# Causal attention: the maxima of the diagonal blocks masked on VectorE instead of by band matmuls on TensorE

## The chip, the core and the metric

The program runs on one core of one Trainium2 chip. The metric is the time of one execution in microseconds of device time, the median of several runs; each comparison is made on one chip. The engines are TensorE (PE in the profile, its weight loads PEld), VectorE (DVE), ScalarE (ACT), GpSimd (POOL) and SyncE (SP), which here only issues DMAs. Each has its own queue, and they wait for one another by semaphores.

## What is computed

Two transformer layers of model width 256 on 4096 tokens: causal attention with 16 heads of 16 dimensions over a 64-wide latent, an MLP with fp4 rounding, full attention, and a coupling network, with a layer norm behind each. The change is in the first attention. Cut to what matters:

```python
def _L0_attn_ref(x, W_q, W_dkv, W_uk, W_uv, W_o, ln_gamma, ln_beta):
    ...                                   # q, k, v: (1, 16, 4096, 16), q and k rotated
    scores = jnp.einsum('bhqd,bhkd->bhqk', q, k) / jnp.sqrt(jnp.float32(HEAD_DIM))
    causal = jnp.tril(jnp.ones((t, t), dtype=bool))
    scores = jnp.where(causal[None, None], scores, -jnp.inf)
    attn = jax.nn.softmax(scores, axis=-1)
    out = jnp.einsum('bhqk,bhkd->bhqd', attn, v)
```

All is float32. The softmax needs each query's maximum over the keys up to its own.

## The kernel before

The function `attention` (L1042) makes both attention layers; `causal` is true for the first. Four heads form a group, 512 queries a block; a **unit** is one block of one group, 32 in the causal layer. The first group takes its blocks from the shortest (512 keys) to the longest (4096), the other three from the longest to the shortest.

For each unit the scores are computed twice. First for the maxima: queries on the partitions, keys along the columns. A **set** is one tile of 128 queries, one pair of heads and 512 keys (`take_max`, L1345): two matmuls (L1353), one for each head of the pair, into two banks of `ps`. VectorE takes the maximum along the columns of both banks in one operation (`reduce_max`, L1503, the reduce at L1506). There are two pairs of banks, used in turn: TensorE waits on `max_taken` until the set two before has been reduced, VectorE on `max_scored`. When all sets of a unit are done, the **gather** (L1510) takes the maximum over the chunks of 512 keys, negates it and splits it in two parts; TensorE turns it (L1363), ScalarE copies it out, and SyncE writes it into extra rows of the queries, so that the second score matmul subtracts it.

Second for the values: keys on the partitions (L1407), `exp` on ScalarE (L1483), and the values matmuls (L1447). A **half-step** is one tile of 128 keys and two of the four heads: two score matmuls, the values matmuls of an earlier tile, and whatever sets of maxima of a coming unit the plan has put between them. The plan (`order`, L1149) is a list that all engines follow; a table of costs (`half_cost`, `max_cost`) spreads the sets over the half-steps so that each unit's maxima are ready some time before the unit begins.

A set is **diagonal** when its keys are those of the unit's own block. Its width is then (qt + 1) x 128 columns for query tile qt, 128 to 512, and in the last 128 columns keys later than the query must not count. Each unit has eight such sets (four tiles, two pairs), and they come last, in a row, ahead of the gather: a **burst**. The band does the masking: after the two score matmuls four more with bfloat16 operands (`add_band`, L1341, the matmul at L1343) add a matrix with -1e30 above the diagonal to those 128 columns, in two halves of 64 rows for each of the two banks:

```python
if diagonal:
    for m in range(2):
        for b in range(2):
            mm = add_band(bank(b)[:, qt * P:wide], b, m)
```

`pick` and `band` are made by GpSimd at the start of the layer (L1277 to L1287), and TensorE waits for them there (`ones_set`, L1367). The probabilities on the diagonal are masked separately, after the exp, by GpSimd (L1293).

Of the kernel before, what the change touches and what calls it, by code (L numbers as in the profile page):

```python
# [1041 lines left out]
def attention(nc, core, ps, ident, layer, causal, q_parts, k_parts, v_dram, K, o_all):  # L1042
# [147 lines left out]
    def par_of(u):  # L1190
        return group_of(u) % 2
# [29 lines left out]
    with ExitStack() as ctx:  # L1221
# [11 lines left out]
        if causal:  # L1233
            pick = sb("pick", [P, 2, P], BF16)
            band = sb("band", [P, 2, P], BF16)

# [36 lines left out]
        with nc.Block() as block:  # L1273
            if causal:
                @block.gpsimd
                def _(pool):
                    pool.memset(band[:], 0.0).then_inc(ones_set, 1)  # L1277
                    pool.memset(pick[:], 0.0).then_inc(ones_set, 1)
                    pool.wait_ge(ones_set, 2)
                    for b in range(2):  # L1280
                        rows = slice(b * HALF, (b + 1) * HALF)
                        for m in range(2):

                            pool.affine_select(out=pick[rows, m], in_=pick[rows, m], compare_op=ALU.not_equal, fill=1.0,
                                               base=m * HALF, pattern=[[-1, P]], channel_multiplier=1).then_inc(ones_set, 1)
                            pool.affine_select(out=band[rows, m], in_=band[rows, m], compare_op=ALU.is_ge, fill=MASKED,
                                               base=m * HALF, pattern=[[-1, P]], channel_multiplier=1).then_inc(ones_set, 1)  # L1287
                    pool.wait_ge(ones_set, 10)
                    for u in range(UNITS):
                        for kt in range(keys(u) - QT, keys(u)):  # L1290
                            pool.wait_ge(emptied, last_score(u, kt) + 4)
                            square = probs[:, (n_key[u] + kt) % PBUFS, :, width(u, kt):width(u, kt) + P]
                            pool.affine_select(out=square, in_=square, compare_op=ALU.is_ge, fill=0.0, base=0,  # L1293
                                               pattern=[[0, GH], [1, P]], channel_multiplier=-1).then_inc(masked, 1)
# [45 lines left out]
            def _(pe):  # L1340
                def add_band(dst, b, m):  # L1341
                    rows = slice(b * HALF, (b + 1) * HALF)
                    return pe.matmul(dst, pick[rows, m], band[rows, m], start=False, stop=(m == 1))  # L1343

                def take_max(i, u, at, pair):  # L1345
# [5 lines left out]
                    for b in range(2):  # L1351
                        rows = slice(b * HALF, b * HALF + SROWS)
                        mm = pe.matmul(bank(b)[:, 0:wide], Q[rows, slot_of(u), j, qt * P:(qt + 1) * P],  # L1353
                                       K[rows, par_of(u), j, c * QB:c * QB + wide], start=True, stop=not diagonal)
                    if diagonal:
                        for m in range(2):
                            for b in range(2):
                                mm = add_band(bank(b)[:, qt * P:wide], b, m)
                    mm.then_inc(max_scored, 1)
# [5 lines left out]
                pe.sem_inc(values_done, PBUFS)  # L1365
                if causal:
                    pe.wait_ge(ones_set, 10)  # L1367
                pe.wait_ge(q_got[slot_of(0)], 96)
# [133 lines left out]
            def _(dve):  # L1502
                def reduce_max(i, u, at, pair):  # L1503
                    j, qt, c = maxima(u)[i]
                    dve.wait_ge(max_scored, at + 1)
                    dve.tensor_reduce(mx[:, u % 2, :, j, qt, c],  # L1506
                                      ps[:, 2 + 2 * pair:4 + 2 * pair, 0:max_width(u, i) // 2], AX.X,
# [771 lines left out]
```

## Time and profile before

| | |
|---|---|
| time, median of 3 runs | 5093.4 us (5091.18 to 5099.55) |
| the profiled execution | 5093.37 us, its span 5091.6 us |
| TensorE busy | 4866.5 us, 96% of the span |
| VectorE busy | 4444.5 us, 87% |
| ScalarE busy | 3780.7 us, 74% |
| GpSimd busy | 376.3 us |
| causal layer | about 160 to 1670 us |
| reduces of the maxima, both layers | 3200, 3729.7 us of VectorE |
| band matmuls | 1024, 80.6 us of TensorE |

The time of an execution is the span, from the first to the last instruction, and a little around it. Busy time of TensorE says less than it seems: its matmuls overlap and their ends are modelled, so the time that a group adds to the program is read from the distance of the steps in the timeline. The same holds on a smaller scale for VectorE, where an operation may start while the one before is still ending: the distance of two starts is the price, the duration is what a waiting engine sees. "Idle before" is the time an engine stood still ahead of an instruction, and behind the arrow stands who ended it.

### The profile page before, as it was taken

The page shows a single profiled execution, that of the slowest core. Times are in us where ns is not written, and L with a number is a line of the kernel's source. Part 1 is how long each engine was busy: PE and PEld are TensorE (multiplying, and loading weights), DVE is VectorE, ACT ScalarE, POOL GpSimd, SP SyncE. Part 2 cuts the span into 40 slices and gives each one's busy share as a digit, 9 for nine tenths or more (in the row PEclk, how much of TensorE's full clock was granted, in tenths as well). Part 3 has the DMA queues.
Part 4 walks back from the last instruction along what each step waited for, and adds up shares of the span by engine and source line. Part 5 has one row for each costly group of instructions (what it writes and reads, how often), then busy time and mean ns, then how long its engine had stood idle before and what let it go on. Part 6 is the DMA issues. An engine that isn't in the chain of part 4 may idle for free. (4 is left out here: it accounts for less than half of the span.)

```text
span 5091.6 us, 102136 instructions
## 1 busy us (share of the span) xinstructions
PE 4866.5 (96%) x42155; PEld 1991.5 (39%) x42155; DVE 4444.5 (87%) x5051; ACT 3780.7 (74%) x7192; POOL 376.3 (7%) x546
## 2 busy tenths in 40 slices
PE   8799999999999899869999999999999999999998
PEld 5333333333334465523333333333333333333443
DVE  7799988988876599489999999999999999998346
ACT  3377888887878433318888888888888888888853
POOL 4100000000000233300000000000000000000120
PEclk9699999999999899959999999999999999999999
DMA  6301010010000000531000010000100000000000
GB/s 192 93 11 38 8 41 8 14 42 11 11 8 2 16 14 8 182 72 37 9 7 5 8 37 9 8 5 8 38 8 8 5 8 5 8 5 2 9 1 33
DMA packets 138405, 131.34 MB, mean 26 GB/s; under 512 B 61748, under 2 KB 96852, under 8 KB 137940
## 3 DMA queue, kind: packets, MB, share of 16 engines
q1 hardware_dynamic: 128964, 118.95, 7.9%
q10 hardware_dynamic: 8976, 5.86, 0.8%
q8 instruction: 332, 5.44, 0.4%
q14 instruction: 133, 1.09, 0.1%
HBM read 76.75 MB, written 46.66 MB: 24 GB/s over the span
## 5 line engine op out<-in xcount | busy, mean ns | idle before, releaser
L1506 DVE TENSOR_REDUCE att_mx<-ps 128x2 f32<-128x1024 f32 (+2 forms) x3200 | 3729.7, 1192 | 252.8 <-PE ps L1353 159.4
L1483 ACT ACTIVATE att_probs<-ps 128x512 f32<-128x512 f32 (+3 forms) x6400 | 3379.8, 583 | 576.0 <-PE ps L1407 262.4
L1447 PE MATMUL ps<-att_probs,att_V 128*17 128x256 f32 (+1 forms) x24576 | 1913.8, 386 | 0.4 <-ACT att_outT L1499 0.2
L1407 PE MATMUL ps<-att_Q,K 50*128 50x512 f32 (+3 forms) x6272 | 1618.1, 490 | 24.1 <-ACT att_probs L1483 23.1
L1353 PE MATMUL ps<-K,att_Q 48*128 48x512 f32 (+3 forms) x6400 | 1364.6, 409 | 83.9 <-DVE att_mx L1506 50.9
L1407 PEld LDWEIGHTS ps<-att_Q,K 50*128 50x128 f32 x6272 | 628.4, 184 | 1320.6 <-ACT att_probs L1483 1227.9
L1447 PEld LDWEIGHTS ps<-att_probs,att_V 128*17 128x17 f32 x24576 | 415.6, 95 | 1025.1 <-issue 564.7
L1353 PEld LDWEIGHTS ps<-K,att_Q 48*128 48x128 f32 x6400 | 645.1, 191 | 166.4 <-DVE att_mx L1506 120.1
L1842 POOL MEMSET mix_power<- 128x1 f32 x1 | 0.1, 99 | 2643.0 <-POOLq L132 2643.0
L1293 POOL TENSOR_SCALAR_AFFINE_SELECT att_probs<-att_probs 128x512 f32<-128x512 f32 x128 | 81.6, 638 | 1454.1 <-ACT att_probs L1483 1454.1
L1634 PE MATMUL ps<-wguT,mlp_xqT 128*128 128x512 f32 (+1 forms) x384 | 159.7, 566 | 0.0
L1673 ACT ACTIVATE mlp_gate<-ps 128x704 f32<-128x704 f32 x32 | 24.2, 757 | 138.8 <-PE ps L1634 138.8
L1462 ACT ACTIVATE att_negT<-ps 32x128 fp32r<-32x128 f32 x65 | 17.2, 265 | 128.4 <-PE ps L1363 123.7
L1541 DVE RECIPROCAL att_rden<-att_out 128x16 f32<-128x16 f32 (+1 forms) x65 | 16.4, 252 | 104.5 <-ACT att_out L1492 104.4
L1634 PEld LDWEIGHTS ps<-wguT,mlp_xqT 128*128 128x128 f32 x384 | 71.8, 194 | 71.8 <-issue 63.3
L1652 PE MATMUL ps<-wdT,mlp_hqT 128*128 128x256 f32 (+1 forms) x384 | 95.6, 391 | 0.6 <-DVE mlp_y L1731 0.6
L2081 PE MATMUL ps<-xT_all,net_w 128*128 128x512 f32 x192 | 95.6, 621 | 0.0
L2029 DVE TENSOR_SCALAR cn_cf<-cn_th,cn_ab 128x512 f32<-128x512 f32 x24 | 13.1, 546 | 83.5 <-ACT cn_th L2163 83.0
L1652 PEld LDWEIGHTS ps<-wdT,mlp_hqT 128*128 128x128 f32 (+1 forms) x384 | 71.0, 192 | 26.3 <-issue 11.6
L1343 PE MATMUL ps<-att_band,att_pick 64*128 64x128 bf16 x1024 | 80.6, 234 | 0.0
L2145 ACT ACTIVATE cn_h<-ps,net_b 128x512 f32<-128x512 f32 x48 | 33.0, 687 | 57.8 <-PE ps L2081 57.8
L591 DVE TENSOR_TENSOR proj_qprod<-ps,proj_tabT 128x1024 f32<-128x1024 f32 x16 | 18.8, 1220 | 50.6 <-PE ps L437 50.6
(213 smaller groups left out, 2463.2 us busy)
## 6 DMA issues: line engine op xcount, KB each, us to landing
att_Q<-qhi_scratch SPq DMA_DIRECT2D x252, 64.0 KB, 2.3
K<-khi_scratch SPq DMA_DIRECT2D x212, 64.0 KB, 2.3
v_scratch<-proj_vpad SPq DMA_DIRECT2D x16, 544.0 KB, 4.4
att_Q<-qlo_scratch SPq DMA_DIRECT2D x126, 64.0 KB, 2.3
att_V<-v_scratch SPq DMA_DIRECT2D x53, 136.0 KB, 2.4
K<-klo_scratch SPq DMA_DIRECT2D x106, 64.0 KB, 2.3
att_Q<-att_negT SPq DMA_DIRECT2D x260, 4.0 KB
proj_x<-in_L_attn_x SPq DMA_DIRECT2D x8, 512.0 KB, 6.2
```

Of the source, the lines that this page charges most:

```text
L1293: pool.affine_select(out=square, in_=square, compare_op=ALU.is_ge, fill=0.0, base=0, pattern=[[0, GH], [1, P]], channel_multiplier=-1).the ...
L1343: return pe.matmul(dst, pick[rows, m], band[rows, m], start=False, stop=(m == 1))
L1353: mm = pe.matmul(bank(b)[:, 0:wide], Q[rows, slot_of(u), j, qt * P:(qt + 1) * P], K[rows, par_of(u), j, c * QB:c * QB + wide], start=True, ...
L1407: mm = pe.matmul(ring(at)[:, lo:QB], K[rows, par_of(u), j, kt * P:(kt + 1) * P], Q[rows, slot_of(u), j, lo:QB], start=True, stop=True)
L1447: mm = pe.matmul(ps[VW * h:VW * h + HV, 6, lo:(part + 1) * (QB // 2)], V[:, par_of(v), kt, HV * h:HV * (h + 1)], probs[:, (n_key[v] + kt) ...
L1483: act.activation(probs[:, (n_key[u] + kt) % PBUFS, h if half_wide(u) else column(h), lo:QB], ring(at)[:, lo:QB], ACT.Exp, scale=SCALE).the ...
L1506: dve.tensor_reduce(mx[:, u % 2, :, j, qt, c], ps[:, 2 + 2 * pair:4 + 2 * pair, 0:max_width(u, i) // 2], AX.X, ALU.max).then_inc(max_taken, 1)
L1634: mm = pe.matmul(gu_ps[:, b:to], xqT[:, par, c, :], wguT[:, c, b:to], start=(c == 0), stop=(c == DC - 1))
L1652: mm = pe.matmul(down, hqT[0:kw, par, k, :], wdT[0:kw, k, :], start=(k == 0), stop=(k == NK - 1))
L1673: act.activation(gate[:], gate_ps, ACT.Silu).then_inc(s["gate_kept"], 1)
L2081: mm = pe.matmul(bank1(k, m), nets.w1[:, c, m * P:(m + 1) * P], xT_all[:, c, cols_of(k)], start=(c == 0), stop=(c == DC - 1))
L2145: act.activation(h1[:, k % 2, m], bank1(k, m), ACT.Gelu, bias=nets.b1[:, m:m + 1]).then_inc(s["hid1"], 1)
```

## The change

The band matmuls and the matrices `pick` and `band` are gone. Instead GpSimd makes one row mask `future` (128 x 512, bfloat16): zero in its first 384 columns and -1e30 above the diagonal of its last 128. For a diagonal set VectorE now runs one `tensor_tensor_reduce` for each of the two banks: it adds the last `wide` columns of `future` to the bank, writes the sum back into the bank and takes its maximum. TensorE signals the set after its two score matmuls. The wait for GpSimd's mask moves from TensorE to VectorE. The other sets, the plan and its costs are as before.

```diff
--- before.py
+++ after.py
@@ -1231,8 +1231,7 @@
         negT = sb("negT", [PARTS * NEG, 2, P], F32R)
         rden = sb("rden", [P, QT, GH])
         if causal:
-            pick = sb("pick", [P, 2, P], BF16)
-            band = sb("band", [P, 2, P], BF16)
+            future = sb("future", [P, QB], BF16)
 
         ones_set = core.sem(pre + "ones_set")
         k_first = [core.sem(f"{pre}k_first_{i}") for i in range(NQB)]
@@ -1274,18 +1273,11 @@
             if causal:
                 @block.gpsimd
                 def _(pool):
-                    pool.memset(band[:], 0.0).then_inc(ones_set, 1)
-                    pool.memset(pick[:], 0.0).then_inc(ones_set, 1)
-                    pool.wait_ge(ones_set, 2)
-                    for b in range(2):
-                        rows = slice(b * HALF, (b + 1) * HALF)
-                        for m in range(2):
-
-                            pool.affine_select(out=pick[rows, m], in_=pick[rows, m], compare_op=ALU.not_equal, fill=1.0,
-                                               base=m * HALF, pattern=[[-1, P]], channel_multiplier=1).then_inc(ones_set, 1)
-                            pool.affine_select(out=band[rows, m], in_=band[rows, m], compare_op=ALU.is_ge, fill=MASKED,
-                                               base=m * HALF, pattern=[[-1, P]], channel_multiplier=1).then_inc(ones_set, 1)
-                    pool.wait_ge(ones_set, 10)
+                    pool.memset(future[:], 0.0).then_inc(ones_set, 1)
+                    pool.wait_ge(ones_set, 1)
+
+                    pool.affine_select(out=future[:, QB - P:QB], in_=future[:, QB - P:QB], compare_op=ALU.is_ge, fill=MASKED,
+                                       base=0, pattern=[[-1, P]], channel_multiplier=1).then_inc(ones_set, 1)
                     for u in range(UNITS):
                         for kt in range(keys(u) - QT, keys(u)):
                             pool.wait_ge(emptied, last_score(u, kt) + 4)
@@ -1338,10 +1330,6 @@
 
             @block.tensor
             def _(pe):
-                def add_band(dst, b, m):
-                    rows = slice(b * HALF, (b + 1) * HALF)
-                    return pe.matmul(dst, pick[rows, m], band[rows, m], start=False, stop=(m == 1))
-
                 def take_max(i, u, at, pair):
                     j, qt, c = maxima(u)[i]
                     pe.wait_ge(max_taken, at + 1)
@@ -1351,11 +1339,7 @@
                     for b in range(2):
                         rows = slice(b * HALF, b * HALF + SROWS)
                         mm = pe.matmul(bank(b)[:, 0:wide], Q[rows, slot_of(u), j, qt * P:(qt + 1) * P],
-                                       K[rows, par_of(u), j, c * QB:c * QB + wide], start=True, stop=not diagonal)
-                    if diagonal:
-                        for m in range(2):
-                            for b in range(2):
-                                mm = add_band(bank(b)[:, qt * P:wide], b, m)
+                                       K[rows, par_of(u), j, c * QB:c * QB + wide], start=True, stop=True)
                     mm.then_inc(max_scored, 1)
 
                 def turn_max(count, at):
@@ -1363,8 +1347,6 @@
                     pe.transpose(ring(at)[:, 0:P], negp[:], ident[:]).then_inc(scored, 1)
 
                 pe.sem_inc(values_done, PBUFS)
-                if causal:
-                    pe.wait_ge(ones_set, 10)
                 pe.wait_ge(q_got[slot_of(0)], 96)
                 keys_here, values_here = set(), set()
 
@@ -1503,6 +1485,16 @@
                 def reduce_max(i, u, at, pair):
                     j, qt, c = maxima(u)[i]
                     dve.wait_ge(max_scored, at + 1)
+                    if on_diagonal(u, c):
+                        if u == 0:
+                            dve.wait_ge(ones_set, 2)
+                        wide = (qt + 1) * P
+                        for b in range(2):
+                            ins = dve.tensor_tensor_reduce(ps[:, 2 + 2 * pair + b, 0:wide], ps[:, 2 + 2 * pair + b, 0:wide],
+                                                           future[:, QB - wide:QB], 1.0, MASKED, ALU.add, ALU.max,
+                                                           mx[:, u % 2, b, j, qt, c:c + 1])
+                        ins.then_inc(max_taken, 1)
+                        return
                     dve.tensor_reduce(mx[:, u % 2, :, j, qt, c],
                                       ps[:, 2 + 2 * pair:4 + 2 * pair, 0:max_width(u, i) // 2], AX.X,
                                       ALU.max).then_inc(max_taken, 1)
```

On VectorE, the first unit's eight diagonal sets at the start of the layer, before (`att_mx` holds the maxima, `att_neg` and `att_negp` the gather's results):

```order
L1506 TENSOR_REDUCE att_mx<-ps 128x2 x8
L1513 TENSOR_REDUCE att_neg<-att_mx 128x16
L1517 CAST att_negp<-att_neg 128x16
L1518 TENSOR_TENSOR att_negp<-att_neg,att_negp 128x16
L1506 TENSOR_REDUCE att_mx<-ps 128x2 x16
```

and now, the last of the eight sets and the gather behind it:

```order
L1493 ISA ps,att_mx<-ps,att_future 128x512
L1493 ISA att_mx 128x1
L1493 ISA ps,att_mx<-ps,att_future 128x512
L1493 ISA att_mx 128x1
L1505 TENSOR_REDUCE att_neg<-att_mx 128x16
L1509 CAST att_negp<-att_neg 128x16
L1510 TENSOR_TENSOR att_negp<-att_neg,att_negp 128x16
L1498 TENSOR_REDUCE att_mx<-ps 128x2 x16
```

The one operation in the code is two instructions in the program, one that reads and writes the bank and one that writes a single column, the maximum: a diagonal set is four instructions where it was one reduce.

On TensorE, in the fifth unit's burst, a half-step with a full set and the two narrowest diagonal sets, before (`K` and `att_Q` are keys and queries, `att_probs` the exponentials):

```order
L1407 MATMUL ps<-att_Q,K 128x512 x2
L1353 MATMUL ps<-K,att_Q 128x512 x2
L1353 MATMUL ps<-K,att_Q 128x128 x2
L1343 MATMUL ps<-att_band,att_pick 128x128 x4
L1353 MATMUL ps<-K,att_Q 128x128 x2
L1343 MATMUL ps<-att_band,att_pick 128x128 x4
L1447 MATMUL ps<-att_probs,att_V 17x256 x4
```

and now:

```order
L1389 MATMUL ps<-att_Q,K 128x512 x2
L1341 MATMUL ps<-K,att_Q 128x512 x2
L1341 MATMUL ps<-K,att_Q 128x128 x4
L1429 MATMUL ps<-att_probs,att_V 17x256 x4
L1389 MATMUL ps<-att_Q,K 128x512 x2
```

Nothing else has moved: the sets stand in the same half-steps, and only the groups of four band matmuls are missing between them.

## Rows read from the trace of the kernel before

**Rows 1.** The page: span; busy us (share of span) xinstructions of each engine
```profile
span 5091.6 us, 102136 instructions
...
PE 4866.5 (96%) x42155; PEld 1991.5 (39%) x42155; DVE 4444.5 (87%) x5051; ACT 3780.7 (74%) x7192; POOL 376.3 (7%) x546
```

**Rows 2.** Busy us by stretches of the causal layer, then granted clock, DMA
```profile
160.00:480.00 320.00, 298.39 (x2654) 122.47 (x2653) 295.51 (x302) 207.47 (x418) 15.30 (x24) 0.89 0.16 39
480.00:1320.00 840.00, 820.77 (x8283) 325.06 (x8283) 751.56 (x747) 682.73 (x1362) 42.76 (x67) 0.99 0.07 19
1320.00:1670.00 350.00, 343.28 (x3375) 137.92 (x3373) 256.66 (x258) 287.78 (x581) 18.48 (x29) 0.98 0.02 6
```

**Rows 3.** Groups by shape, 160 to 1670 us: busy, mean ns | idle before
```profile
L1506 DVE TENSOR_REDUCE att_mx<-ps 128x2 f32<-128x1024 f32 x960 | 1140.5, 1223 | 122.6 <-PE ps L1353 100.2 <-PE ps L1343 18.6
...
L1343 PE MATMUL ps<-att_band,att_pick 64*128 64x128 bf16 x1021 | 80.4, 234 | 0.0
...
L1506 DVE TENSOR_REDUCE att_mx<-ps 128x2 f32<-128x768 f32 x64 | 60.3, 957 | 24.2 <-PE ps L1343 23.8
...
L1506 DVE TENSOR_REDUCE att_mx<-ps 128x2 f32<-128x256 f32 x64 | 26.9, 423 | 15.2 <-PE ps L1343 15.0
```

**Rows 4.** Waits, 160 to 1670 us: who for whom, total us, times, longest
```profile
DVE att_mx L1506 <- PE ps L1343: 87.2, 137, 8.5
...
PE ps L1353 <- DVE att_mx L1506: 26.6, 55, 1.1
```

**Rows 5.** Timeline, TensorE, unit 8's burst: start, us, instructions [idle before]
```profile
574.94 0.33 PE L1353 MATMUL ps<-K,att_Q 48*128 48x128 f32 x2 [0.76 <-DVE att_mx L1506]
...
580.01 0.51 PE L1407 MATMUL ps<-att_Q,K 50*128 50x512 f32 x2
...
581.37 0.50 PE L1407 MATMUL ps<-att_Q,K 50*128 50x512 f32 x2
...
582.73 0.50 PE L1407 MATMUL ps<-att_Q,K 50*128 50x512 f32 x2
...
583.95 0.50 PE L1407 MATMUL ps<-att_Q,K 50*128 50x512 f32 x2
...
585.56 0.49 PE L1353 MATMUL ps<-K,att_Q 48*128 48x512 f32 x2
```

**Rows 6.** Timeline of VectorE, the same burst and behind its gather
```profile
568.76 6.46 DVE L1506 TENSOR_REDUCE att_mx<-ps 128x2 f32<-128x1024 f32 x6 [1.17 <-PE ps L1353]
...
580.92 2.58 DVE L1506 TENSOR_REDUCE att_mx<-ps 128x2 f32<-128x1024 f32 x2 [0.40 <-PE ps L1343]
...
584.28 5.75 DVE L1506 TENSOR_REDUCE att_mx<-ps 128x2 f32<-128x1024 f32 x5
```

**Rows 7.** Timeline of VectorE, unit 7's burst
```profile
485.51 8.56 DVE L1506 TENSOR_REDUCE att_mx<-ps 128x2 f32<-128x1024 f32 x8
...
497.22 4.29 DVE L1506 TENSOR_REDUCE att_mx<-ps 128x2 f32<-128x768 f32 x4 [0.61 <-PE ps L1343]
```

**Rows 8.** Timeline of TensorE, behind unit 7's gather
```profile
503.57 0.49 PE L1353 MATMUL ps<-K,att_Q 48*128 48x512 f32 x2
```

**Rows 9.** Timeline of VectorE, short operations of the MLP
```profile
1901.69 0.43 DVE L1731 TENSOR_TENSOR mlp_y<-ps,a_all 128x256 f32<-128x256 f32 x1 [0.42 <-PE ps L1652]
1902.03 0.41 DVE L1731 TENSOR_TENSOR mlp_y<-ps,mlp_x 128x256 f32<-128x256 f32 x1
...
1903.24 0.27 DVE L1741 TENSOR_SCALAR mlp_var<-mlp_mv 128x1 f32<-128x1 f32 x2
1903.44 0.89 DVE L174 TENSOR_REDUCE mlp_qh_amax<-mlp_h 128x44 f32<-128x704 f32 x1
```

**Rows 10.** Timeline of all engines, the start of the causal layer
```profile
151.10 0.48 DVE L1522 MEMSET ps<- 128x512 f32 x1
...
153.29 0.30 POOL L1286 TENSOR_SCALAR_AFFINE_SELECT att_band<-att_band 64x128 bf16<-64x128 bf16 x1
...
159.31 0.47 PE L1353 MATMUL ps<-K,att_Q 48*128 48x128 f32 x2 [11.03 <-DMA K<-khi_scratch]
```

## Prediction

> **What bounds the kernel now.** I read the page first [rows 1]: TensorE is busy 96% of the span, VectorE 87%, ScalarE 74%. That is an average over stages, so next came the busy time by stretches [rows 2]. The change touches only the causal layer, which runs from 160 to about 1670 us. In its first 320 us VectorE is busy 296 of 320 us and TensorE 298; from 480 to 1320 TensorE has 821 of 840 and VectorE 752; in the last 350 us VectorE has 257 and TensorE 343. So TensorE sets the pace, and VectorE is close behind it until 1320. The granted clock is 0.89, 0.99 and 0.98 there; I assume that it stays so.
>
> Then the groups of the layer by shape [rows 3]: 960 full reduces of 1223 ns, and 64 each for three, two and one quarter of the width, 957 to 423 ns. The 256 diagonal sets are those 192 and 64 of the full ones. The band's 1021 recorded matmuls are 80.4 us busy, but busy is not cost here, since matmuls overlap. The waits [rows 4] show both sides: VectorE waited 87.2 us for the band's line (137 times, 8.5 us of it once, at the start), TensorE 26.6 us for VectorE's reduces. Diagonal sets come eight in a row, one burst in each of 32 units, and what the change does is decided inside the bursts and just behind them.
>
> **What the band costs TensorE.** In the timeline of unit 8's burst [rows 5] a half-step (two score matmuls, one set of maxima, eight values matmuls) with a full-width diagonal set runs from 580.01 to 581.37 and from 581.37 to 582.73: 1.36 us. The next one, without a band, 582.73 to 583.95, takes 1.22. So a band of four matmuls costs 0.14 us of TensorE's pace, a sixth of what 4 x 234 ns suggests; 256 sets give 36 us. That is the most that the change can take off.
>
> **What VectorE gets.** One reduce over two banks becomes, by the built order, four instructions: per bank an add-and-maximum and a one-column write of its result. No row of before shows either, so both are bounded by neighbours, in start-to-start time, since that is what a queue of them costs. The reduces: five full ones in a row take 5.75 us [rows 6], so they start (5.75 - 1.22)/4 = 1.13 apart although each lasts 1.22; a quarter more, 2 x 128 columns, costs 0.267 (1223 - 957) [rows 3]. So the old sets cost 0.33, 0.60, 0.87 and 1.13, and a burst 5.86. Nearest to the new main instruction is the tensor-tensor that reads a bank: 256 columns, 0.43 long, the next starts 0.34 later (1901.69, 1902.03) [rows 9]; with the same slope that is 0.21, 0.34, 0.47 and 0.61 for 128 to 512 columns. Nearest to the one-column write are the one-column tensor-scalars: two of them, and the next row starts 0.20 later (1903.24, 1903.44), 0.10 each [rows 9]. Bounds: from below 0.06, if a write without an input is cheaper than these; from above each instruction at its full length, no overlap, 0.16 fixed for a main one (0.43 - 0.267) and 0.15 for a write (0.27 for two that overlap). I take 0.34 and 0.10, the rows nearest in shape. A set then costs 2 x (bank + 0.10) = 0.61, 0.88, 1.15, 1.41, a burst of eight 8.10: **2.24 us more per unit**, 72 us over the stage. VectorE's waits in the bursts, 87.2 - 8.5 = 79 us, are of that size: it can be carried, if it falls in the right places.
>
> The Trainium skill ("VectorE: DVE Perf Modes", Rules for kernel authors) asks to keep the number of VectorE operations low and speaks against turning one into four. Its page on this has no price for the second instruction; nothing below needs it.
>
> **Two bursts worked through.** Rules, from the rows: TensorE writes a set 0.05 after the reduce two sets earlier has ended (two pairs of banks); VectorE may start 0.04 after the last matmul; a reduce's end is seen 0.08 after the next may start.
> Unit 8 [rows 5, 6]: the first diagonal reduce starts at 574.80, inside the row of six. With the new costs the eight start at 574.80, 575.41, 576.34 (waits for its matmuls), 577.22, 578.10, 579.25, 580.40, 581.81 and the last ends at 583.30, against 583.50. TensorE, without bands, starts the half-step behind the burst at 581.78 instead of 582.73: it is 0.95 ahead. But the gather (0.77 from the last reduce to the first full one) now starts with VectorE a set behind, the first full reduce ends at 585.28, and TensorE's third set behind the burst, which needs its banks, goes at 585.33 instead of 585.56. Of 1.1 us saved 0.23 is left: **-0.23**.
> Unit 7 [rows 7, 8] is denser: the planner, whose costs are unchanged, puts three small sets in one half-step and the last four reduces run without a gap. The same working gives 493.66, 494.27, 494.88, 495.83, 496.98, 498.13, 499.28, 500.69, an end at 502.18 (before about 501.51), a first full reduce until 504.16, and TensorE's write at 504.21 instead of 503.57: **+0.64**.
>
> **The sum.** Counting the 32 bursts of the timeline by VectorE's idle time in them: 11 are like unit 8 (1.9 to 2.7 us idle), 8 like unit 7 (1.4 to 1.5), 2 (the first units of the last two head groups) have 0.9 and lose about 1.1 each. The first four units run at a lower clock, where the band is dearer and VectorE waits 1.2 to 3.2 us; I put them at 0, give or take 2. In the last seven VectorE has room (257 of 350 us, [rows 2]) and most of 8 x 0.14 stays, 0.9 each. 11 x -0.23 + 8 x 0.64 + 2 x 1.1 + 0 - 7 x 0.9 = -2.5 + 5.1 + 2.2 - 6.3 = **-1.5 us**.
> Edits at nothing: the mask's preparation on GpSimd shrinks from ten operations to two, but it was done by 153.6 and the first maxima matmul at 159.31 waited for a key load [rows 10]; without that load it would save about 2 us. The wait for it moves to VectorE, which has nothing to do then. The second layer, projections and MLP are unchanged.
> The profiled execution took 5093.37 us with a span of 5091.6, the median is 5093.4: so 5093.4 - 1.5 = **5092 us**.
> Sensitivity: some 25 bursts have 16 pairs each, so 0.01 us more per pair costs up to 4 us. With 0.08 for the write it is 5084, with 0.12 5100.
>
> **Rivals.**
> 1. *Not slower, but faster: VectorE's room suffices.* If the one-column write is nearly free (0.06 and less, as a write without input), a unit-8 burst leaves TensorE 0.9 us ahead and a unit-7 burst is even. 16 us and more off; at the limit all 36: 5058 to 5082, say 5074. The point from which it decides is about 0.08 per write. For it: the 79 us of waits. Against: the one-column rows that there are take 0.10.
> 2. *Slower: the four instructions don't overlap.* A write of the accumulated maximum may hold the next until the main one has drained. Then each pair costs 0.08 + 0.05 more, 25 x 16 x 0.13 = 52 us, less what bursts with room absorb: **5144**; half of it (only the write waits) 5115. For it: the write depends on the instruction ahead of it, which no pair in [rows 9] does. Against: every row of VectorE shown overlaps its successor by about 0.08. The Trainium skill says two things here ("VectorE: DVE Perf Modes"): under The DRAIN you can't avoid, that the next operation waits until the pipe is empty, which would be this rival; under Two Vector instructions with no wait between them, that one which isn't held starts earlier, which is my forecast. The five reduces 1.13 apart side with the second, for reduces.
> 3. *Reading and writing the same bank halves the rate.* Nothing in before does both. A unit's eight sets hold 2560 columns in two banks each, 2560 x 1.04 ns x 2 = 5.3 us more: some 28 bursts, 150 us, 5240. Against: the one VectorE write into a bank takes 0.48 us for 512 columns [rows 10], no slower than a read.
>
> **How the numbers follow.** About 0.2% (10 us) is what a measurement of this kernel can tell from no change. Forecast (within 0.2%, 5083 to 5104): 0.40. Rival 1: 0.26. Rival 2 from its half on, with prices between: 0.29. Rival 3: 0.05. The range runs from 5070 to 5148: it leaves out rival 3, the deep end of rival 1 and a tail of rival 2, some 0.18. So faster 0.26, same 0.40, slower 0.34.
>
> **What would show it.** Two new groups on VectorE, 512 each: a main one of about 0.29 to 0.69 us and a one-column one whose successor starts 0.10 later (right), 0.06 or less (rival 1), 0.15 and more or with gaps (rival 2); a main one of 512 columns over 1.1 us is rival 3. VectorE's busy time in the layer should rise by 70 to 100 us. TensorE's half-steps with a full diagonal set should be 1.22 where VectorE keeps up; its waits for VectorE's line, 26.6 us, should grow to some 40 to 60, right behind the gathers. If they stay at 27, the write is cheap; if they pass 90, rival 2 or 3 holds. The prediction is wrong altogether if the last 350 us of the layer don't get shorter, since there TensorE alone should decide.

## The result: 0.2 to 0.4% slower, because TensorE's granted clock fell

The changed kernel takes 5125.2 us in the median of 5 runs (5113.4 to 5130.1) against 5093.4 of 5 runs before: ratio 1.0043, 95% interval 1.0022 to 1.0064. Ten more runs of it, beside 22 of before, gave 5115.2 us and 1.0021 (1.0007 to 1.0034). The forecast was 5092, within 0.2%. Four runs of the experiments, far above the others of their kernel (5166 us in e1, 8147 in e10, 10099 in e3, 12741 in e13), are left out of every figure below. The profiled execution took 5113.4 us. Its page (span; then busy us, share, instructions) answers to [rows 1]:

```profile
span 5111.7 us, 100847 instructions
...
PE 4872.8 (95%) x41131; PEld 1972.0 (39%) x41131; DVE 4483.7 (88%) x5819; ACT 3781.4 (74%) x7192; POOL 373.5 (7%) x538
```

The 1024 band matmuls are gone, VectorE has 39 us more, TensorE 6 us more busy time although it does less. The stretches of the layer, as in [rows 2], the granted clock third from the end:

```profile
160.00:480.00 320.00, 292.70 (x2346) 114.53 (x2345) 295.40 (x462) 199.78 (x404) 15.23 (x24) 0.85 0.17 39
480.00:1320.00 840.00, 815.61 (x7573) 310.77 (x7571) 760.26 (x1139) 673.32 (x1334) 38.72 (x61) 0.96 0.07 19
1320.00:1670.00 350.00, 341.90 (x3180) 133.57 (x3176) 275.26 (x429) 287.76 (x584) 19.67 (x31) 0.97 0.03 7
```

0.89, 0.99 and 0.98 have become 0.85, 0.96 and 0.97. The records of the granted clock know two levels only, 2.4 and 1.2 GHz: stretches at the lower one that begin between 160 and 1690 us add up to 58 us before and 154 us after. The second layer and the MLP are as they were.

**What VectorE does now** (groups by shape, 160 to 1691 us: busy, mean ns of one | idle before), for [rows 3]:

```profile
L1498 DVE TENSOR_REDUCE att_mx<-ps 128x2 f32<-128x1024 f32 x896 | 1062.9, 1222 | 114.2 <-PE ps L1341 112.7
L1493 DVE CUSTOM_DVE_ANT_0 ps<-ps,att_future 128x512 f32<-128x512 f32 x128 | 85.4, 724 | 11.8 <-PE ps L1341 10.8
L1493 DVE DVE_READ_ACCUMULATOR2_ANT att_mx<- 128x1 f32 x512 | 72.4, 141 | 0.0
...
L1493 DVE CUSTOM_DVE_ANT_0 ps<-ps,att_future 128x128 f32<-128x128 f32 x128 | 33.8, 314 | 8.6 <-PE ps L1341 8.3
```

What counts in a queue is the distance of the starts. In unit 8's burst (timeline, VectorE: start, us):

```profile
583.29 0.29 DVE L1493 CUSTOM_DVE_ANT_0 ps<-ps,att_future 128x128 f32<-128x128 f32 x1
...
588.71 0.70 DVE L1493 CUSTOM_DVE_ANT_0 ps<-ps,att_future 128x512 f32<-128x512 f32 x1
589.33 0.14 DVE L1493 DVE_READ_ACCUMULATOR2_ANT att_mx<- 128x1 f32 x1
589.33 0.73 DVE L1493 CUSTOM_DVE_ANT_0 ps<-ps,att_future 128x512 f32<-128x512 f32 x1
589.98 0.14 DVE L1493 DVE_READ_ACCUMULATOR2_ANT att_mx<- 128x1 f32 x1
589.98 0.73 DVE L1493 CUSTOM_DVE_ANT_0 ps<-ps,att_future 128x512 f32<-128x512 f32 x1
```

The one-column read starts together with the next main instruction. From main to main it is 0.65 us at 512 columns, and over all pairs 0.25, 0.38, 0.52 and 0.65 us for 128 to 512. The trace does not divide a pair between its two instructions; it is 0.04 us over the price that the prediction gave the main instruction alone, so with that price the read costs 0.04, not 0.10. A burst is 7.2 us, not 8.1.

**And TensorE in that burst** (timeline):

```profile
589.16 0.50 PE L1389 MATMUL ps<-att_Q,K 50*128 50x512 f32 x2
...
590.37 0.50 PE L1389 MATMUL ps<-att_Q,K 50*128 50x512 f32 x2
...
591.59 0.50 PE L1389 MATMUL ps<-att_Q,K 50*128 50x512 f32 x2
...
593.47 0.50 PE L1341 MATMUL ps<-K,att_Q 48*128 48x512 f32 x2 [0.16 <-DVE att_mx L1498]
```

Half-steps with a full diagonal set take 1.21 and 1.22 us, as forecast. From the first diagonal instruction on VectorE (583.29) to TensorE's third set behind the burst it is 10.18 us, against 10.76 in [rows 5, 6] (574.80, inside the row of six, to 585.56): 0.58 us gained. Here the clock is at its full level throughout (columns as in [rows 2]):

```profile
580.00:597.00 17.00, 15.85 (x155) 6.04 (x151) 16.28 (x43) 13.33 (x27) 0.59 (x1) 1.00 0.01 1
```

So in this burst the work itself got cheaper, and the time went elsewhere.

**Where it went.** Gathers mark the units. The gathers of units 23 and 24 before (timeline, VectorE):

```profile
1233.59 0.18 DVE L1513 TENSOR_REDUCE att_neg<-att_mx 128x16 f32<-128x16 f32 x1
...
1318.59 0.29 DVE L1513 TENSOR_REDUCE att_neg<-att_mx 128x16 f32<-128x128 f32 x1
```

and after:

```profile
1249.83 0.18 DVE L1505 TENSOR_REDUCE att_neg<-att_mx 128x16 f32<-128x16 f32 x1
...
1342.49 0.29 DVE L1505 TENSOR_REDUCE att_neg<-att_mx 128x16 f32<-128x128 f32 x1
```

The distance grew from 85.0 to 92.7 us. In this run the 7.7 us fall together with one long stretch at the lower clock, shown here with a shorter one ahead of it (busy time by stretches of after; columns as in [rows 2]):

```profile
1228.00:1231.40 3.40, 2.40 (x24) 1.00 (x26) 2.90 (x11) 1.48 (x4) 0.00 (x0) 1.00 0.00 0
1231.40:1238.20 6.80, 6.80 (x46) 2.29 (x38) 4.43 (x17) 4.08 (x8) 0.00 (x0) 0.50 0.01 2
...
1248.40:1251.80 3.40, 2.83 (x28) 1.16 (x20) 3.26 (x11) 2.94 (x6) 0.00 (x0) 1.00 0.45 113
1251.80:1275.70 23.90, 23.90 (x133) 7.93 (x133) 13.36 (x13) 12.82 (x25) 0.00 (x0) 0.50 0.01 3
```

At both falls TensorE had just paused: 2.40 of 3.40 us busy, then 2.83 of 3.40. At half clock it is busy without a gap, and the others wait for it (VectorE is busy 13.4 of 23.9 us). The Trainium skill ("TensorE: Matmul & The Clock Gate", What's actually happening) says that the gate between the two levels follows how busy the array has been; these rows agree as far as the falls stand behind pauses; that the clock stayed low through 23.9 us without a gap does not fit it, and here the measurement decides. Pauses alone are not enough, either. At the same places of the program, ahead of the gather of unit 22 and behind that of unit 23 (1240.5 and 1249.8 us in after, 1224.6 and 1233.6 in before), the kernel before pauses nearly as much and keeps its clock:

```profile
1214.00:1217.40 3.40, 2.53 (x32) 1.29 (x28) 2.80 (x4) 1.52 (x3) 0.00 (x0) 1.00 0.00 0
...
1234.40:1237.80 3.40, 2.93 (x23) 1.14 (x21) 3.31 (x3) 3.28 (x8) 0.00 (x0) 1.00 0.09 29
```

**Time against clock.** Each run has its mean granted clock beside its time, and the runs of one kernel differ in both. The 135 runs of before that went with the experiments reach from 5083.9 us at 0.968 to 5130.2 us at 0.958. One straight line with a common slope and a level for each of the 19 kernels fits 301 runs to 3.2 us (the spread around it): **3.9 us for 0.001 of clock**. That splits each difference into what the work costs at an equal clock (0.962, by the line) and what the clock adds. Times and clocks below are medians; each ratio is to the runs of before on the same chip. "Two-byte" counts the matmuls in the band's form and type. The experiments ran at six times on five chips, each time beside before, whose mean clock came out at 0.964 or 0.965 and whose level by the line at 5112 to 5118 us; so differences of level below some 6 us between kernels of different times say little.

| kernel | two-byte matmuls | plan | us | ratio (95%) | clock | us at 0.962 |
|---|---|---|---|---|---|---|
| before | 1024 | old | 5103.0 | 1 | 0.965 | 5114 |
| after (15 runs) | 0 | old | 5117.7 | 1.0043, 1.0021 | 0.958 | 5103 |
| e1 no band, old reduces | 0 | old | 5094.3 | 0.9989 (0.9970 to 1.0008) | 0.960 | 5087 |
| e2 band and new reduces | 1024 | old | 5117.4 | 1.0030 (1.0012 to 1.0047) | 0.963 | 5122 |
| e3 after, planned | 0 | new | 5089.8 | 0.9977 (0.9963 to 0.9991) | 0.961 | 5086 |
| e4 before, half band | 512 | old | 5110.7 | 1.0013 (0.9990 to 1.0037) | 0.960 | 5104 |
| e5 as e1, half reduces | 0 | old | 5078.5 | 0.9954 (0.9930 to 0.9978) | 0.962 | 5080 |
| e6 e3 + 2 score-like on diagonal | 0 | new | 5114.7 | 1.0027 (1.0006 to 1.0049) | 0.960 | 5108 |
| e7 e3 + 2 score-like elsewhere | 0 | new | 5109.1 | 1.0009 (0.9982 to 1.0035) | 0.961 | 5105 |
| e8 after + band in ten units | 320 | old | 5129.2 | 1.0035 (1.0014 to 1.0057) | 0.958 | 5113 |
| e9 e3 + band in ten units | 320 | new | 5093.1 | 0.9979 (0.9964 to 0.9993) | 0.964 | 5101 |
| e10 after + 4 score-like (3 runs) | 0 | old | 5219.4 | 1.0238 (1.0175 to 1.0301) | 0.943 | 5148 |
| e11 e3 + 4 zeros on diagonal | 1024 | new | 5094.3 | 0.9991 (0.9976 to 1.0007) | 0.966 | 5110 |
| e12 e3 + 4 zeros elsewhere | 896 | new | 5091.6 | 0.9985 (0.9968 to 1.0001) | 0.9665 | 5110 |
| e13 after, planned wider | 0 | wider | 5088.7 | 0.9971 (0.9953 to 0.9990) | 0.963 | 5092 |
| e14 e3 + 2 zeros elsewhere | 448 | new | 5096.1 | 0.9976 (0.9958 to 0.9994) | 0.963 | 5101 |
| e15 e3 + 4 short zeros elsewhere | 896 | new | 5091.0 | 0.9971 (0.9949 to 0.9992) | 0.964 | 5099 |
| e16 e3 + 4 four-byte zeros elsewhere | 0 | new | 5130.2 | 1.0043 (1.0021 to 1.0066) | 0.9595 | 5120 |
| e17 after + 4 zeros elsewhere | 896 | old | 5142.9 | 1.0062 (1.0044 to 1.0079) | 0.958 | 5126 |

At an equal clock the change gains 5114 - 5103 = 11 us (13 in the ten runs of e0 against the runs of before beside them). Its clock is 0.0066 lower in the mean (0.9580 of 15 runs, 0.9646 of 135), which costs 26 us.

### The profile page after: what moved, and what is told of

Its sections match the earlier page's. It is cut to its first block and busy times, and to the rows that moved or that the text cites. A ratio compares the mean times of both kernels' runs of the same rounds, so it can differ in the third digit from the quotient of the medians.

```text
span 5111.7 us, 100847 instructions
## 1 busy us (share of the span) xinstructions
PE 4872.8 (95%) x41131; PEld 1972.0 (39%) x41131; DVE 4483.7 (88%) x5819; ACT 3781.4 (74%) x7192; POOL 373.5 (7%) x538
## 5 line engine op out<-in xcount | busy, mean ns | idle before, releaser
L1498 DVE TENSOR_REDUCE att_mx<-ps 128x2 f32<-128x1024 f32 x2944 | 3525.8, 1224 | 175.1 <-PE ps L1341 172.0
L1429 PE MATMUL ps<-att_probs,att_V 128*17 128x256 f32 (+1 forms) x24576 | 1933.4, 389 | 0.2
L1493 DVE CUSTOM_DVE_ANT_0 ps<-ps,att_future 128x384 f32<-128x384 f32 (+3 forms) x512 | 237.2, 520 | 57.4 <-PE ps L1341 55.4
L1493 DVE DVE_READ_ACCUMULATOR2_ANT att_mx<- 128x1 f32 x512 | 72.4, 141 | 0.0
```

The source lines that it names most:

```text
L1429: mm = pe.matmul(ps[VW * h:VW * h + HV, 6, lo:(part + 1) * (QB // 2)], V[:, par_of(v), kt, HV * h:HV * (h + 1)], probs[:, (n_key[v] + kt) ...
L1493: ins = dve.tensor_tensor_reduce(ps[:, 2 + 2 * pair + b, 0:wide], ps[:, 2 + 2 * pair + b, 0:wide], future[:, QB - wide:QB], 1.0, MASKED, A ...
L1498: dve.tensor_reduce(mx[:, u % 2, :, j, qt, c], ps[:, 2 + 2 * pair:4 + 2 * pair, 0:max_width(u, i) // 2], AX.X, ALU.max).then_inc(max_taken, 1)
```

## Experiments: which part of the change moves the clock

**e0**, the changed kernel again.

> The changed kernel itself, for the spread of its granted clock over more runs. If its slowness is the clock: single runs spread over 30 us or more and each lies on one line of time against clock, 3.9 us for 0.001; the median clock is 0.954 to 0.959, that of before 0.965. If the first five runs were chance: a median clock of 0.962 or above and 5085 to 5105 us.

5105.3 to 5129.5 us, clock 0.955 to 0.962, median 0.9595: a spread of 24 us, not 30, and a median clock just above what was expected of the first theory, well below the 0.962 of the second. The slowness stands, and the runs lie on the common line of time against clock.

**e1 and e2** take the two halves of the change apart. e1 removes the band and leaves VectorE its old reduces; e2 keeps the band and has the new instructions.

```diff
 e1: after, and in reduce_max
-                    if on_diagonal(u, c):
...
-                        return
 e2: before, and in reduce_max
+                    if on_diagonal(u, c):
...
+                        return
```

> The band's matmuls are gone and VectorE keeps its old reduces; the diagonal sets' maxima are taken without the mask, which is left out. Before has a mean granted clock of 0.968, after 0.954 to 0.959. Theory P (pauses: the changed reduces hold TensorE up in the bursts, and its granted clock falls behind such pauses): nothing is added on VectorE, so the clock stays at 0.965 or above and 20 to 36 us come off, 5057 to 5073. Theory A (activity: the band's matmuls filled TensorE, and taking them away is what lowers the clock): the clock falls to 0.955 to 0.96 as in after, which takes 25 to 40 us back, 5075 to 5100. Theory V (VectorE's extra time alone costs the 20 to 30 us and the clock does not matter): 5057 to 5073, as P.

> The band's matmuls stay and VectorE takes the masked maxima in the new way as well (the mask is added twice, which leaves the probabilities as they are). Theory P: VectorE's longer bursts meet TensorE's longer ones, the pauses are like those of after or more, the clock falls to 0.96 or below, 5125 to 5160. Theory A: the band keeps the clock at 0.965 or above; the new reduces alone cost 0 to 0.6 us a unit, 5093 to 5112. Theory V: the clock stays at 0.965 or above and the time is 5130 to 5160, the extra of VectorE on top of the whole band.

e1: clock 0.960, 5094 us. Taking the band away lowers the clock with VectorE's work untouched: theory A, against P and V. At an equal clock the band is worth 5114 - 5087 = 27 us. e2: clock 0.963, between what A and P expected; the new instructions cost 5122 - 5114 = 8 us at an equal clock and some 0.001 of clock. TensorE's waits for VectorE do not separate the two (160 to 1690 us: us, times, longest). In e1:

```profile
PE ps L1341 <- DVE att_mx L1488: 30.0, 62, 1.3
```

and in e2:

```profile
PE ps L1358 <- DVE att_mx L1521: 25.7, 52, 1.1
...
PE ps L1358 <- DVE att_mx L1516: 4.6, 11, 0.6
```

30.0 and 30.3 us, and yet the profiled runs have 140 us at the lower clock in e1 and 48 in e2. Around the gather of unit 22 (1235.2 us in e2), where after fell first, e2 pauses about as much, twice, and holds (busy time by stretches):

```profile
1224.20:1227.60 3.40, 2.54 (x34) 1.13 (x28) 3.36 (x10) 1.75 (x4) 0.00 (x0) 1.00 0.00 0
...
1234.40:1237.80 3.40, 2.59 (x38) 1.29 (x38) 3.15 (x16) 1.53 (x4) 0.64 (x1) 1.00 0.03 7
```

**e3 and e13** tell the planner what a diagonal set costs now; e13 tells it more than that.

```diff
     def max_cost(u, i):
-        return 0.155 + max_width(u, i) / 960
+        return (0.31 if on_diagonal(u, maxima(u)[i][2]) else 0.155) + max_width(u, i) / 960
...
 e13: 0.6 in place of 0.31
```

> The changed kernel with one more fixed cost of 0.155 us for each diagonal set in the planner that spreads the sets over the half-steps (measured start distances of a pair, 0.249, 0.382, 0.515 and 0.649 us, make a set 0.50 to 1.30 us). A burst is then spread over more half-steps and VectorE is pressed less there. Theory P: fewer pauses, the clock goes back to 0.962 or above, 5065 to 5095. Theory A: as after, 0.954 to 0.959, 5113 to 5130. Theory V: TensorE waits less, 5080 to 5110 at an unchanged clock of 0.954 to 0.959.

> The changed kernel with a fixed cost of 0.6 us for each diagonal set in the planner in place of 0.31: the bursts are spread still wider, and VectorE has more room in them. Theory P (TensorE's pauses behind VectorE start the falls): fewer waits for VectorE, clock 0.962 or above, 5078 to 5090. Theory S: the clock stays at 0.961 and the time within 4 us of 5090, or above it, since the sets between the bursts are then closer together.

e3: 5089.8 us, faster than before by 0.23%. At an equal clock it is where e1 is (5086 and 5087, each to some 2 us): with bursts spread by their new price, the masked reduces cost no more than the old ones did in the old plan. (The old reduces were not run in the new plan.) The clock came half way, 0.961: spreading counts (P), but does not make up for the band. e13 has 0.963 and 5088.7, at an equal clock 6 us more than e3: it seems to gain clock and lose pace, but the two were run at different times, and the differences are at the edge of what can be told.

**e4 and e5.** Half of the band; and e1 with half of the columns reduced.

```diff
 e4: before, and in take_max
-                        for m in range(2):
+                        for m in range(1, 2):
 e5: e1, and in reduce_max
-                                      ps[:, 2 + 2 * pair:4 + 2 * pair, 0:max_width(u, i) // 2], AX.X,
+                                      ps[:, 2 + 2 * pair:4 + 2 * pair, 0:max_width(u, i) // (4 if on_diagonal(u, c) else 2)], AX.X,
```

> The kernel before with two of the four band matmuls of each diagonal set (the mask of the maxima reaches half of the query rows; the other half's maxima are taken unmasked). VectorE's work is as in before. Theory A (the band's matmuls keep TensorE's granted clock up; without them it fell to 0.960 in the median, with them 0.966): half of them hold it about half way, 0.962 to 0.964, and half of the 29 us that the band costs at an equal clock comes off: 5090 to 5102. Theory P (pauses behind VectorE lower the clock): as before, 0.966 and 5075 to 5087, since VectorE has no more to do. Theory N (the clock falls by chance, whatever the kernel): no order between the kernels' clocks.

> No band, and VectorE reduces only half of the columns of each diagonal set (the rest of these maxima is left out, and the mask): TensorE is not held up by VectorE inside a burst. Theory A: the clock stays low, 0.955 to 0.961, since TensorE has no more to do than without the band, 5075 to 5100. Theory P: the pauses are gone, the clock is 0.966 or above, 5050 to 5065.

e4 missed: its clock is not half way but at 0.960, though single runs reach 0.968. e5 has 0.962: relieving VectorE in the bursts gives back about 0.002, so pauses look like a smaller part, and without the band the clock does not return to 0.965.

**e6, e7, e10.** Is any matmul as good as the band's? Matmuls like those of the scores, on the set's own bank ahead of the real ones, overwritten by them; e6 and e10 on the diagonal, e7 off it.

```diff
+                    if diagonal:
+                        for b in range(2):
+                            rows = slice(b * HALF, b * HALF + SROWS)
+                            pe.matmul(bank(b)[:, 0:P], Q[rows, slot_of(u), j, qt * P:(qt + 1) * P],
+                                      K[rows, par_of(u), j, c * QB:c * QB + P], start=True, stop=True)
...
 e7: if causal and not diagonal and qt == 0; e10: the pair twice, old plan
```

> The changed kernel with the planner's new cost (median 5090 us at a clock of 0.9615), and in each diagonal set two more matmuls of 128 columns ahead of the real ones, whose results are overwritten (512 more matmuls, half as many as the band had). Theory A, any matmul counts: the clock comes back to 0.964 or above, which gives 10 to 15 us, and the matmuls cost about half of the band's 29 us: 5088 to 5096. Theory B (the band's own form counts): the clock stays at 0.961 and the matmuls' price is seen alone, 5100 to 5110.

> As the one before, but the two overwritten matmuls of 128 columns stand in the first quarter of the sets off the diagonal (224 sets, 448 matmuls), so away from the bursts where the band stood. Theory A, any place counts: the clock rises to 0.963 or above, 5085 to 5097. If only matmuls in the bursts count: the clock stays at 0.961 and the price is seen alone, 5098 to 5108.

> The changed kernel with four matmuls of 128 columns ahead of the real ones in every diagonal set, overwritten by these: as many as the band had, in its bursts, but in the form of the score matmuls. With the band itself in the same place the clock was 0.963 and the time 5117. Theory A1 (the number of matmuls in the bursts counts): clock 0.962 or above, 5117 to 5135. Theory A2 (the band's own form counts): clock 0.954 to 0.959, 5135 to 5165.

None brings the clock back: 0.960, 0.961, and 0.943 in the three runs of e10, below all others. Theory A in the form "any matmul counts" falls, and the times lie above the ranges given. Why e10 fell so far is open. In its profiled run the end of the causal layer, whose last gather is at 1752.5 us, ran almost wholly at the lower clock, 85 us in one stretch:

```profile
1690.00:1780.00 90.00, 88.35 (x588) 38.14 (x580) 24.80 (x80) 49.45 (x111) 8.88 (x14) 0.54 0.01 2
```

**e8 and e9.** The band beside VectorE's mask in ten units only.

```diff
+    def banded(u, c):
+        return on_diagonal(u, c) and (chunks(u) <= 2 or u <= 3)
...
-                    if diagonal:
+                    if banded(u, c):
```

> The changed kernel with the band's four matmuls kept besides (mask added twice) in the ten units that have at most two chunks of keys, or that are the third and fourth: 80 of 256 diagonal sets. Long stretches at the lower clock began at the ends of head groups, at 862 and 1234 us, where these units' bursts lie close together. Theory A (the band fills TensorE where it would pause, and the clock holds): the clock rises from 0.956 to 0.960 or above, and the band costs 8 us: 5108 to 5120. Theory B (the band has to stand everywhere): clock 0.954 to 0.959, 5120 to 5140.

> The same with the planner's new cost for diagonal sets (without the band: median 5090 us, clock 0.961). Theory A: clock 0.964 or above, 5078 to 5090, below every kernel so far. Theory B: clock 0.959 to 0.962, 5094 to 5102.

With the new plan the clock rises from 0.961 to 0.964, with the old one the median stays at 0.958 (the mean goes from 0.9580 to 0.9594). The time is no better, since the band costs what the clock gives.

**e11, e12, e16.** The band's matmuls without a mask: four that add zero, on the diagonal (e11) or in the first quarter of the sets off it (e12); in e16 as in e12, but with four-byte operands.

```diff
+                    if diagonal:
+                        for m in range(2):
+                            for b in range(2):
+                                rows = slice(b * HALF, (b + 1) * HALF)
+                                mm = pe.matmul(bank(b)[:, 0:P], future[rows, 0:P], future[rows, P:2 * P], start=False, stop=(m == 1))
...
 e12: if causal and not diagonal and qt == 0; e16: as e12, with a tile of four-byte zeros for future
```

> The changed kernel with the planner's new cost, and in each diagonal set four matmuls in the band's form (added to the set, 128 columns, two-byte operands) that add zero: the band's work without its mask. Without them: median 5090 us at 0.961. Theory F (matmuls in the band's form and place hold the clock): 0.964 or above; at an equal clock the band costs 26 us, so 5098 to 5108. Theory S (they do not; what holds the clock in the kernel before is that VectorE waits for the band, or chance): 0.959 to 0.962, 5110 to 5122.

> The same four matmuls that add zero, but in the first quarter of the sets off the diagonal (224 sets, 896 matmuls) and none on it. Theory F with the form alone: 0.964 or above, 5095 to 5105. Theory F with the place (only where bursts press VectorE): 0.959 to 0.962, 5108 to 5120. Two score-like matmuls in these places left the clock at 0.961.

> The four matmuls of zeros of 128 columns with operands in the type of the score matmuls (four bytes) in place of two bytes. If adding to a bank (not overwriting) or adding zeros is what holds the clock: 0.965 or above, 5090 to 5105. If the two-byte type is what holds it: 0.960 to 0.962, and the price of four-byte matmuls, 5110 to 5160.

The clearest answer of all: 0.966 and 0.9665, no run of either below 0.963, wherever the zeros stand; and 0.9595 for the same matmuls with the wider type. (Both zeros kernels are a little faster than theory F expected.) The groups of e12 and of e16 (busy us, mean ns) show that the wide ones keep TensorE busy no less:

```profile
L1347 PE MATMUL ps<-att_future 64*128 64x128 bf16 x896 | 71.0, 226 | 0.0
```

```profile
L1349 PE MATMUL ps<-att_nothing 64*128 64x128 f32 x896 | 85.2, 256 | 0.0
```

A part of the 256 ns is e16's lower clock itself. At an equal clock the wide zeros cost 34 us over e3, the two-byte ones 24.

**e14 and e15**: two zeros in place of four; four of 32 columns.

```diff
 e14: e12 with
-                        for m in range(2):
+                        for m in range(1):
 e15: e12 with
-                                mm = pe.matmul(bank(b)[:, 0:P], future[rows, 0:P], future[rows, P:2 * P], start=False, stop=(m == 1))
+                                mm = pe.matmul(bank(b)[:, 0:32], future[rows, 0:P], future[rows, P:P + 32], start=False, stop=(m == 1))
```

> As the kernel with matmuls of zeros off the diagonal, but two of them in each of the 224 sets in place of four. Four held the clock at 0.9665 and cost 24 us at an equal clock. If the clock follows their number: 0.963 to 0.965, 5088 to 5096. If two are enough: 0.966 and 5078 to 5088. If two do nothing: 0.961 and 5098 to 5106.

> Four matmuls of zeros in each of the 224 sets, but of 32 columns in place of 128. If their number and their weight loads count: clock 0.965 or above, 5080 to 5092. If the columns that they stream count: 0.961 to 0.963, 5090 to 5106.

0.963 and 0.964, between none (0.961) and four (0.9665): the clock follows their amount. So does the price, 15 and 13 us at an equal clock against 24. Neither their number nor their columns alone orders the three: e15 has e12's 896 matmuls and a quarter of its columns, e14 half of both, and their mean clocks are 0.9630 and 0.9634. No amount is a gain that could be told: e3, e9 and e11 to e15 all end between 5089 and 5096 us.

**e17**: e12's zeros in the changed kernel with its old plan (e12's edit alone).

> The changed kernel itself, the planner untouched, with the four two-byte matmuls of zeros in each of the 224 sets off the diagonal. The changed kernel alone had 0.956 and 0.9595 in the median and lies at 5103 us at a clock of 0.962; the zeros cost 24 us at an equal clock. If the missing two-byte matmuls are what lowered the clock of the changed kernel: 0.964 or above, 5105 to 5122. If its dense bursts lower it by themselves: 0.957 to 0.961, 5128 to 5148.

0.958: the second expectation. In the dense bursts of the old plan, zeros that stand elsewhere do not hold the clock; in e2 the band inside the bursts did (0.963). From 160 to 1690 us, the whole layer in e12 (last gather at 1668.5) and all but its end in e17 (1721.0): e12, with the new plan,

```profile
160.00:1690.00 1530.00, 1480.64 (x14342) 593.22 (x14343) 1348.46 (x2072) 1193.94 (x2397) 81.23 (x128) 0.96 0.08 20
```

and e17:

```profile
160.00:1690.00 1530.00, 1481.15 (x13907) 590.08 (x13910) 1332.27 (x2009) 1153.87 (x2307) 73.61 (x116) 0.93 0.08 20
```

**What is settled:** the clock alone turns a gain of 11 us into a loss; two parts of the change lower it, the missing band (before to e1; that its two-byte type counts was shown with the new plan only, by e11 and e12 against e3 and e16) and bursts that the planner leaves too dense (after to e3; e12 to e17). **What stays open:** why matmuls of two-byte operands hold the clock and four-byte ones do not, and why in the old plan only those inside the bursts do. How dense bursts lower the clock is open too: TensorE's waits for VectorE are 30.5 us in e12 and 32.0 in e17 (profiled runs, 160 to 1690 us), nearly the same. e4 and e8 lie lower than the amount of their matmuls would put them. Place may count: in the profiled runs two of the three longest low stretches of e17 begin around the ends of head groups (873.1 and 1255.4 us), where units are short and its zeros are fewest, as do two of after's (876.4 and 1251.8); e8, with its band just there, has its long ones elsewhere. But e0, the same kernel as after, has none there either, so this is a guess.

## Why the prediction was wrong, step by step

- *"The granted clock is 0.89, 0.99 and 0.98 there; I assume that it stays so."* This step failed, and by itself decides the sign: the mean clock of the execution fell from 0.9646 to 0.9580, and 0.0066 of clock is 26 us that the sum had at nothing. No rival had it. That the time came out near the half of rival 2 (5115) is chance, since rival 2 did not happen.
- *Band: 0.14 us a set, 36 us at most.* Right in kind: half-steps of 1.22 us came, and at an equal clock e1 gains 27 us; 36 counted every band at TensorE's pace; where the other 9 us stayed, no run shows.
- *A one-column write costs 0.10.* Mis-sized: a pair takes 0.25 to 0.65 us, 0.06 less than the 0.31 to 0.71 of the sum, which leaves 0.04 for the write if the main instruction was right (only the pair is measured). A burst has 1.3 us more, not 2.24. By this price alone rival 1 holds ("0.06 and less"), and VectorE's 39 us more instead of 70 to 100 and unit 8's 0.58 us instead of 0.23 agree with it.
- *Two bursts by hand, sum -1.5 us.* At an equal clock it is -11. The stated sensitivity, 4 us for 0.01 of a write, would give 24 us more than the forecast; with the old plan less than half of that is left, and the new plan (e3) collects it: 28 us below before.
- *TensorE's waits for VectorE should grow from 26.6 us to 40 to 60.* They did, although the price came out lower: after's waits (160 to 1691 us):

```profile
PE ps L1341 <- DVE att_mx L1498: 31.9, 66, 1.3
...
PE ps L1341 <- DVE att_mx L1493: 8.6, 25, 0.6
```

40.5 us. A small part of the rise comes from the faster TensorE alone (e1, with the old reduces, has 30.0), the rest came with the new instructions. So this sign, meant to tell a dear write from a cheap one, did not.
- *The last 350 us of the layer must get shorter.* From the gather of unit 24 to the last: 351.1 us before, 348.0 after (1342.5 to 1690.5). Half of the 6.3 us, at a clock of 0.97 instead of 0.98.
- *Rival 2, four instructions that wait for each other.* Excluded by the starts 0.65 apart of instructions that last 0.73. Of the two rules weighed there, the Trainium skill's page "VectorE: DVE Perf Modes" is borne out in its section Two Vector instructions with no wait between them, which also says that an operation with an accumulator output counts as two instructions: the trace has four to a set. *Rival 3, half rate in a bank:* 0.72 us for 512 columns, not over 1.1.

## What to carry to other kernels

Where TensorE sets the pace, the granted clock is a term of the sum: read it by stretch, and if an edit takes matmuls out or makes TensorE pause, say what the clock will do, with a price taken from runs (here 3.9 us for 0.001). Compare kernels at an equal clock before explaining a difference of half a per cent, since otherwise a true gain of work looks like a loss. And when the price of a step changes, give it to the planner: here that one line was worth 17 us at an equal clock in the changed kernel, more than the change itself (the new plan was not tried in the kernel before).

## What the runs showed of the hardware

- Matmuls of zeros with two-byte operands, 896 in 1.5 ms, raised the mean granted clock from 0.961 to 0.9665 (e3, e12); the same with four-byte operands left it at 0.9595, though TensorE was busy with them no less (e16: 256 against 226 ns each). In the old plan the two-byte zeros did not raise it (0.958 in after and in e17).
- Once at the lower level the clock can stay there while TensorE is busy without a gap: 23.9 us in after (23.90 of 23.90 us busy). The longest stretch in the layer behind its first 60 us was 13.7 us before, 17.1 at its very end; in e1 34.1.
- The accumulator's read takes 141 ns by its record and starts together with the next main instruction in a queue; a main instruction and its read, from start to start, take 0.25, 0.38, 0.52 and 0.65 us for 128 to 512 columns.
